# Linear attention with a feed-forward layer: all small matmuls of a slot in one group, with the product with the state behind the scores

## The reference

```python
q, k, v = x @ Wq.T + bq, x @ Wk.T + bk, x @ Wv.T + bv     # split into 16 heads of 32
q, k = exp(q), exp(k)
kv, k1 = cumsum(k[..., :, None] * v[..., None, :]), cumsum(k)      # along the sequence
att = (einsum('zsD,zsDd->zsd', q, kv) / sum(q * k1, -1)) @ Wo.T + bo
x = layernorm(x + att)
x = layernorm(x + tanh(x @ weight @ aux_weight1 @ aux_weight2 + bias))
```

## Time and profile before

| | |
|---|---|
| median of 3 runs | 2325.98 us (2323.97 to 2326.26) |
| profiled execution, its own time | 2327.15 us |
| its span, first to last instruction | 2325.3 us |
| PE busy | 2263.8 us (97%) |
| DVE, POOL, ACT busy | 1575.0, 1460.9, 1024.5 us |
| mean granted clock of TensorE | 0.994 |

### The profile page before, as it was taken

The page is one execution under the profiler, slowest core; times in us unless marked ns, Lnnn a source line. Parts: engine busy times, 40 slices in busy tenths (PEclk is TensorE's granted clock), DMA queues, the critical chain, the costliest instruction groups (busy, mean ns, idle before and its releaser), DMA issues.

```text
span 2325.3 us, 70786 instructions
## 1 busy us (share of the span) xinstructions
PE 2263.8 (97%) x27752; PEld 1824.1 (78%) x27752; DVE 1575.0 (68%) x2316; ACT 1024.5 (44%) x1683; POOL 1460.9 (63%) x1925
## 2 busy tenths in 40 slices
PE   3999999999999999999999999999999999999996
PEld 3788888888888888888888888888888888888874
DVE  3566776776776776776776776776676676676675
ACT  2444444444444444444444444444444444444443
POOL 1266666666666666666666666666666666666565
PEclk9999999999999999999999999999999999999998
DMA  6233333333333333333333333333333333333222
GB/s 160 62 106 109 111 102 110 109 103 107 111 102 109 110 102 106 113 102 108 111 102 107 112 102 109 111 101 106 114 101 108 112 101 107 113 102 109 75 62 67
DMA packets 294451, 242.73 MB, mean 104 GB/s; under 512 B 33328, under 2 KB 225840, under 8 KB 294192
## 3 DMA queue, kind: packets, MB, share of 16 engines
q1 hardware_dynamic: 294192, 238.69, 33.6%
HBM read 139.99 MB, written 98.57 MB: 103 GB/s over the span
## 4 chain that ended last, share of the span: by engine, by line
PE 96%; DVE 1%; DMA 1%; ACT 1%; SPq 0%; POOL 0%; issue 0%; POOLq 0%; DVEq 0%; ACTq 0%
PE G L310 27%; PE G L311 25%; PE G L312 25%; PE SC L367 6%; PE SC L402 6%; PE SC L395 3%; PE SC L390 2%; PE G L414 2%; DVE o L679 1%; PE SC L310 0%; PE SC L312 0%; PE SC L311 0%; DMA KT<-wkT 0%; DMA QT<-wqT 0%; SPq L271 0%
## 5 line engine op out<-in xcount | busy, mean ns | idle before, releaser
L700 POOL TENSOR_SCALAR_AFFINE_SELECT A<-A 128x512 f32<-128x512 f32 x512 | 380.8, 776 | 480.4 <-ACT A L501 480.3
L501 ACT ACTIVATE A<-SC 128x512 f32<-128x512 f32 x512 | 264.3, 605 | 390.8 <-PE SC L367 390.8
L626 DVE TENSOR_TENSOR WK<-G,bfbc 128x512 f32<-128x512 f32 x128 | 88.6, 692 | 505.8 <-PE G L312 505.8
L679 DVE RECIPROCAL o<-SC 128x512 f32<-128x512 f32 x128 | 428.6, 3348 | 2.7 <-PE SC L402 2.4
L530 ACT ACTIVATE WK<-xres,shift,rstd 128x512 f32<-128x512 f32 x128 | 104.4, 816 | 463.7 <-POOL shift L727 463.7
L746 POOL TENSOR_TENSOR oL<-o,oH 128x512 fp32r<-128x512 f32 x128 | 165.7, 1294 | 158.5 <-ACT oH L545 158.5
L310 PE MATMUL G<-xTH,WqH 128*128 128x512 f32 x512 | 214.8, 420 | 27.0 <-POOL xTL L713 27.0
L713 POOL TENSOR_TENSOR xTL<-xin,xTH 128x512 fp32r<-128x512 f32 x128 | 163.2, 1276 | 103.2 <-ACT xTH L516 103.2
L310 PE MATMUL G<-WvH,xTH 128*128 128x512 f32 x512 | 214.2, 418 | 0.0
L632 DVE TENSOR_TENSOR_SCAN WK<-ones,k,KT 128x128 f32<-128x128 f32 x512 | 212.0, 477 | 0.0
L310 PE MATMUL G<-WfH,x1H 128*128 128x512 f32 x512 | 200.9, 392 | 9.2 <-issue 8.4
(11 more groups left out here) (100 smaller groups left out, 4962.6 us busy)
## 6 DMA issues: line engine op xcount, KB each, us to landing
xin<-x SPq DMA_DIRECT2D x512, 64.0 KB, 2.5
xres<-x SPq DMA_DIRECT2D x128, 256.0 KB, 2.9
x_rows<-WK SPq DMA_DIRECT2D x128, 256.0 KB, 2.1
WK<-x_rows SPq DMA_DIRECT2D x512, 64.0 KB, 2.0
out<-WK SPq DMA_DIRECT2D x128, 256.0 KB, 3.0
k_rows<-WK SPq DMA_DIRECT2D x120, 256.0 KB, 2.0
WK<-k_rows SPq DMA_DIRECT2D x480, 64.0 KB, 2.0
QT<-wqT SPq DMA_DIRECT2D x4, 256.0 KB, 4.3
```

The costliest lines, as they stand in the source:

```text
L501: nc.scalar.activation(A[:, j, :, :].rearrange("p g q -> p (g q)"), SC[:, j, :], ACT.Copy).then_inc(scores_out[j], 1)
L679: nc.vector.reciprocal(o[:, :, :], den_ps).then_inc(recip_ready, 1)
L700: last = nc.gpsimd.affine_select(out=A[:, j, :, :], in_=A[:, j, :, :], compare_op=ALU.is_ge, fill=0.0, base=0, pattern=[[0, NK], [1, P]], ...
```

## The change

PSUM is laid out anew. `SC` (four banks) now holds the scores and all five large products: q and the feed-forward in bank 0, k in bank 1, v in bank 2, the output projection in bank 3. A second tensor `ND` of four banks holds numerators, denominators and the state update, and the products of the start. A has two copies, one for even and one for odd tiles.

On PE the denominators, the product with the state and the masked product of a tile move into the next slot, and the state update a slot later as well. The slot begins with all small groups in a row: denominators of k-1, scores of k, product with the state of k-1, masked product of k-1, state update of k-2. The large ones follow: q, k, v, output projection of k-1, feed-forward of k-2; where no q and k are left, the feed-forward comes ahead of the output projection. The waits follow the banks: the scores wait until each of the four banks has been read, and each large product waits until ScalarE has copied that bank's scores.

```diff
-        A = sb("A", [P, HG, NK, P])
+        A = sb("A", [P, 2, HG, NK, P])
-        G = [ctx.enter_context(nc.psum_tensor(f"G{i}", [P, D], F32)) for i in range(4)]
-        num_ps, den_ps = SC[:, :, 0:P], SC[:, :, P:2 * P]
-        state_ps, kproj_ps = G[0], G[0]
-        oproj_ps, ffn_ps = G[1], G[1]
-        qproj_ps = G[2]
-        v_ps = G[3]
+        ND = ctx.enter_context(nc.psum_tensor("ND", [P, HG, NK * P], F32))
+        num_ps, den_ps = ND[:, :, 0:P], ND[:, :, P:2 * P]
+        state_ps = ND[:, 0, 2 * P:3 * P]
+        qproj_ps, kproj_ps, v_ps, oproj_ps, ffn_ps = SC[:, 0, :], SC[:, 1, :], SC[:, 2, :], SC[:, 3, :], SC[:, 0, :]
...
@@ PE, slot(c, k)
+                if prev:
+                    wait_before(pe, (qk1_ready, c.count(k)), (o_ready, c.count(k - 1)),
+                                (state_ready, c.state_count(k - 2)))
+                    for g, j, quarter, h in heads:
+                        last = nc.tensor.matmul(den_ps[quarter, j, :], ones[h, :], qk1[h, g, :], start=True, stop=True)
+                    last.then_inc(den_done, 1)
                 if att:
                     wait(pe, k_ready, c.quad_count(k))
                     wait(pe, q_ready, c.quad_count(k))
-                    wait(pe, o_ready, c.count(k))
+                    wait(pe, z_ready, c.count(k - 2))
+                    wait(pe, k_ready, c.count(k + 4))
+                    wait(pe, v_ready, c.count(k))
+                    wait(pe, r_ready, c.count(k - 1))
                     for g, j, _, h in heads:
                         last = nc.tensor.matmul(SC[:, j, g * P:(g + 1) * P], KT[h, s, g, cols],
                                                 QT[h, s, g, cols], start=True, stop=True)
                     last.then_inc(scores_done, 1)
+                if prev:
+                    if c.reads_state(k - 1):
+                        for g, j, quarter, h in heads:
+                            nc.tensor.matmul(num_ps[quarter, j, :], state[h, (k - 1) % B, g, :], QT[h, ps, g, pcols],
+                                             start=True, stop=False, skip_group_check=True)
                     wait(pe, v_ready, c.count(k))
-                    three_pass(v_ps[:, :], ...)            
...
+                    wait(pe, masked, c.count(k))
                     for j in range(HG):
                         for g in range(NK):
...
-                if c.updates_state(k - 1):
-                    n = k - 1
+                if c.updates_state(k - 2):
+                    n = k - 2
...
+                    if att:
+                        wait(pe, scores_out[0], c.count(k + 1))
                     wait(pe, q_ready, c.count(k + 4))
...
-                if ffn:
-                    ...
-                    wait(pe, r_ready, c.count(k))
-                    three_pass(ffn_ps[:, :], ...)
+                if att:
+                    wait(pe, scores_out[2], c.count(k + 1))
+                    three_pass(v_ps, ...).then_inc(v_done, 1)
+                if ffn and not proj:
+                    feed_forward()
+                if prev:
+                    output_projection()
+                if ffn and proj:
+                    feed_forward()
```

More of the change, by code:

```diff
@@ L272, in slot @@
                                      x_b[n % B, c.it + n // B, j]).then_inc(xin_loaded[n % B], 16)
[L273 to L279, removed]
[L280 to L283 removed]
+                if c.exists(k - 2):
+                    n = k - 2
                     wait_before(sp, (x1_stored[n % B], c.dma_count(n)), (x1l_ready, c.count(n)))
@@ L695, in slot @@
                 fin = c.exists(k - 3)
-                if att:
-                    for j in range(HG):
-                        wait_before(pool, (scores_out[j], c.count(k + 1)))
-                        last = nc.gpsimd.affine_select(out=A[:, j, :, :], in_=A[:, j, :, :], compare_op=ALU.is_ge,
-                                                       fill=0.0, base=0, pattern=[[0, NK], [1, P]],
-                                                       channel_multiplier=-1)
-                    last.then_inc(masked, 1)
                 if fin:
@@ L707, in slot @@
                     nc.gpsimd.tensor_tensor(y[:, n % 2, :], y[:, n % 2, :], x1[:, n % 2, :], ALU.add).then_inc(y_ready, 1)
+                if att:
+                    for j in range(HG):
+                        wait_before(pool, (scores_out[j], c.count(k + 1)))
+                        last = nc.gpsimd.affine_select(out=A[:, k % 2, j, :, :], in_=A[:, k % 2, j, :, :],
+                                                       compare_op=ALU.is_ge, fill=0.0, base=0,
+                                                       pattern=[[0, NK], [1, P]], channel_multiplier=-1)
+                    last.then_inc(masked, 1)
@@ new lines, in slot @@
+                if prev:
+                    wait(pool, oh_ready, c.count(k))
+                    wait(pool, oproj_done, c.count(k - 1))
+                    nc.gpsimd.tensor_tensor(oL[:, :, :], o[:, :, :], oH[:, :, :].bitcast(F32),
+                                            ALU.subtract).then_inc(ol_ready, 1)
+                if ffn:
+                    wait(pool, x1h_ready, c.count(k - 1))
+                    halves = [t[:, :, :].rearrange("p g (t q) -> p g t q", q=HD) for t in (x1H, x1L)]
+                    nc.gpsimd.tensor_tensor(halves[1], x1s[:, :].rearrange("p (t g q) -> p g t q", t=HG, q=HD),
+                                            halves[0].bitcast(F32), ALU.subtract).then_inc(x1l_ready, 1)
@@ L708, in slot @@
+                if att:
+                    if not prev:
+                        pool.wait_ge(c_ready, 1)
+                    wait(pool, xres_loaded[k], c.dma_count(k))
+                    nc.gpsimd.tensor_tensor(xres[:, k % 2, :], xres[:, k % 2, :], cbc[:, :],
+                                            ALU.add).then_inc(xb_ready, 1)
                 if c.exists(k + 8):
```

291 lines of the change are left out of this document (142 added, 149 removed).

## The result

The changed kernel takes 2485.44 us (median; 2478.12 to 2492.58) against 2324.97 us for the kernel before in the same runs: a ratio of 1.069, with an interval of 1.0671 to 1.0709. The direction was as predicted; the time lies 39 us above the upper end of the range. The profiled execution took 2486.89 us, its span 2485.1 us, at a mean granted clock of 0.978.

The account below looks back on a forecast made before the run. PE was taken to bound the kernel, 96% of the chain that ended last. 2327 us plus 46 in the body and 50 at the end gave 2423, rounded to 2420 us, slower by 4%; range 2372 to 2446.

Parts of the forecast that it names:

- What bounds the kernel, and the slot of large work: Body: PE bounds the kernel; the 60 large matmuls of a slot take 13.48 us from first to last start.
- The wait for z: Body: scores wait for DVE's addition reading bank 0, a 0.52 us stall; slot 17.83 us, 0.38 more, 46 us in all.
- The upper bound's term: Body: changing from scores to the product with the state might cost 0.15 us more, making the slot's increase 0.55 us.
- Nothing else should be late in the body: Body: oL and x1L come 1.5 and 2.9 us early, and DVE is free for z; no further cost.
- Rival (c): Body: x1's reload or busy DVE comes late, a second wait; 121 us per microsecond per slot, 2540 us; chance 0.05.
- The DMA queue: Body: x1's store and reload take 5.4 us against some 7.4 available; beyond 2.9 us late, every slot would pay.
- The end: Last slots: feed-forward waiting for x1 holds the next output projection, a loop of 22.6 us against 13.15; 50 us together.
- (a): Rival: only the body pays, the end absorbs the later x1; 2373 us, chance 0.07.
- (b): Rival: only the end pays, 36 to 49 us, and the scores don't stall; 2346 to 2376 us, chance 0.07.
- (d): Rival: faster; the scores' wait is covered and the last slots stay at 13.15 us; 2310 us, chance 0.03.
- (e): Rival: only the order changes, stall and saved boundary cancel; 2326 us, chance 0.02.
- The grouping's own gain: Body: small groups in one run save 0.14 us per slot if nothing waits, 17.31 against 17.45; 17 us in all.

Follow-up runs that it names:

- e1: The changed kernel with the constant 1 of the four scans read from a spare PSUM column instead of SBUF; 2432.94 us, ratio 1.0459.
- e3: The changed kernel with the output projection ahead of the feed-forward in the last slots too; 2462.95 us, ratio 1.0582.
- e6: e1 with the product with the state moved ahead of the scores, between denominators and scores; 2365.15 us, ratio 1.0169.
- e7: The changed kernel with the scans moved earlier on DVE, ahead of the second norm's statistics, their constant still in SBUF; 2638.07 us, ratio 1.1341.

## Why the prediction was wrong

- **What bounds the kernel, and the slot of large work**: right. The large run was worked out at 13.48 us and measured 13.49.
- **The wait for z**: mechanism right, price a little high. A slot with the shortest wait takes 17.69 us, not 17.83: 1.32 to the scores (1.26 forecast; DVE's release took 0.21 us instead of 0.14), 1.11, then the product with the state in 0.43 instead of 0.68, as it now follows the scores, 0.90, 0.44, and 13.49. Against the 17.42 of before that is 0.27 x 121 = 33 us in place of 46. The upper bound's term, a cost of changing from the scores to the product with the state, did not show: 1.11 us against 1.10. (The bounds' own terms give 0.28 and 0.53, written there as 0.30 and 0.55; nothing hangs on it.)
- **"Nothing else should be late in the body"**: this step failed. I worked DVE forward with the durations of its old rows and concluded that "DVE is free for z"; the four scans, between the turn of x1 and the residual's addition, do not stand in that working at all. At their old price, 1.60 us for four, they would have fitted, as they do in e1. But they were measured where they began with GpSimd idle, and the new order starts them under oL, x1L, the residual's addition and the split of x. They became 575 ns longer in the mean, some 2.3 us per slot, and DVE is late to z in half of the slots. e1 gives the price: 2216.7 - 2161.4 = 55 us; its 2432.94 us lie inside the predicted range. Rival (c) named "DVE comes late to z", as a matter of its load, and got 0.05. Its size of 1 us per slot was twice the measured 0.46.
- **The DMA queue**: right that x1's reload has cover enough; e1 shows it.
- **Code**: not in the prediction. 21 us in e1. That they come from the loads is inferred, and that after pays the same is assumed: between 200 and 2300 us its trace has only 13 gaps of the kind of which e1 has 23. That 33 + 21 + 55 give the body's 109 confirms nothing, since the 55 and the 21 are, by how they were formed, what is left of the 109.
- **The end**: right. 48 us for 50; slots of 21.35, 21.54 and 22.65 us for 21.8, 22.6 and 22.6, and 68.5 us behind the scores of tile 127 for 68.9, the half clock as counted, and the idle time 4.8 to 4.9 us for "over 5". e3 confirms the loop, by 22 us; the other 26 were left when the loop was cut, with PE waiting for the output projection instead.
- **Start**: 3.5 us instead of about 1.
- **Rivals**: (a), (b), (d) and (e) are excluded by 109 us in the body and 48 at the end. The range's upper end had room for the stall's price, but none for a second lateness in the body.
- **The grouping's own gain**: forecast 0.14 us per slot if nothing waited. e6, where nothing waits, shows 0.18 to 0.2 (17.24 against 17.42 to 17.45), so that order does pay, once the wait is covered. But it is not the order forecast: the array changes its shape four times per slot in e6, five times before and after. No run tells whether the gain comes from gathering the groups or from one change less.

## What to carry to other kernels

A duration read from a trace belongs to its neighbours: before moving an instruction on DVE that reads two SBUF operands, look up what GpSimd will be doing when it begins in the new place, and add what is then left of GpSimd's instruction; here a constant operand in PSUM took the scan out of the conflict. Where a bank's reader gates a group, put into the gap a group that doesn't need the bank (e6), and watch the last slots, where a chain that was hidden by other work becomes a loop. If small matmuls are gathered into one long run, shift the code by a few KB before believing a difference of 2%.

## What the runs showed of the hardware

- A scan of 128x128 that reads two operands in SBUF takes some 453 ns when it begins with GpSimd idle, even if a GpSimd addition begins during it. One that begins under a GpSimd instruction ends 0.28 us behind it: 1.45 to 1.47 us in the mean under x1L, the residual's addition or the split of x (after), 788 ns under a mask (e7). With one of the operands in PSUM (e1) the 267 scans that began under oL took 453 ns and the 91 that began under x1L 459.
- The other way round the price was smaller: in the kernel before, the 131 masks that began under a scan took 777 ns, where the median of the others is 631.
- Instructions are loaded 16,384 bytes at a time (235 loads in e1). 64 more instructions of PE at the start cost the body of e1 46.6 us, 128 more gave back 7.0, and the kernel before did not notice them.
- An idle time of 4.9 us of PE was followed by a stretch of 5.40 us, with the twelve matmuls, at a granted clock of 0.55; in the 5.00 us behind it the clock was 1.00.
